# Routed experts on one core: the search for the k-th score, the first row lists and the row gathers, in another order

## What is computed

```python
h = _layernorm(x) * (1 + ca) + sa
x = x + ga * causal_mean(h)              # softmax over an all-zero causal mask
h = _layernorm(x) * (1 + cb) + sb        # the token rows, here called h2
x = x + gb * ffn(h)
# ffn: 8 experts, width 128 -> 512 -> 128, gelu
scores = softmax(xf @ gate_weight.T).T                       # 8 x 4096
vals, idx = top_k(scores.reshape(-1), 2 * S)                 # the 8192 best pairs
gate = zeros(8, S).at[idx // S, idx % S].add(vals)
out = einsum('es,esd->sd', gate, y) + shared                 # y: each expert's output
```

## Time and profile before

| | us |
|---|---|
| median of 3 runs (404.95 to 410.02) | 405.38 |
| the profiled execution | 403.75 |
| its span in the profile | 402.0 |
| busy: PE / DVE / ACT / POOL | 297.1 / 168.1 / 138.1 / 209.7 |
| POOL, scatters L779 (72) | 113.5 |
| POOL, gathers L766 (72) | 69.9 |

### The profile page before, as it was taken

One profiled execution on the slowest core, in us unless ns is written; L12 is line 12 of the kernel. 1 busy time (PEld: TensorE's weight loads), 2 busy tenths in 40 slices (PEclk: granted clock), 3 DMA queues, 4 the chain that ended last, 5 costly groups with the idle time before them and its releaser, 6 DMA issues.

```text
span 402.0 us, 4835 instructions
## 1 busy us (share of the span) xinstructions
PE 297.1 (74%) x1158; PEld 162.7 (40%) x1158; DVE 168.1 (42%) x774; ACT 138.1 (34%) x228; POOL 209.7 (52%) x216
## 2 busy tenths in 40 slices
PE   1647667799999699998776977679786897669500
PEld 1536657653334344544332543335343344234200
DVE  2777748247775860244344213442144323211200
ACT  2135546743334235433233333233232333233200
POOL 2333443100000065037878788787888788786662
PEclk9998665569999999999899889898899989898955
DMA  8907200230000095044455554555445555342331
GB/s 231 294 2 201 62 27 30 68 48 0 27 28 27 26 277 147 28 127 87 76 118 126 105 102 82 115 126 106 100 82 119 125 103 104 74 73 27 30 34 13
DMA packets 49886, 35.96 MB, mean 89 GB/s; under 512 B 7816, under 2 KB 44479, under 8 KB 49855
## 3 DMA queue, kind: packets, MB, share of 16 engines
q0 software_dynamic: 13824, 14.46, 21.1%
q1 hardware_dynamic: 35792, 20.73, 18.5%
q10 hardware_dynamic: 238, 0.42, 0.4%
HBM read 23.65 MB, written 11.94 MB: 89 GB/s over the span
## 4 chain that ended last, share of the span: by engine, by line
POOL 34%; PE 23%; issue 17%; DMA 11%; DVE 11%; ACT 1%; SPq 1%; POOLq 0%; DVEq 0%; ACTq 0%
POOL out_dram L779 23%; POOL R L766 9%; PE Y L916 8%; DMA out_dram<-YO,IDXB 8%; PE U L892 7%; DVE R L434 2%; DMA XW<-in_L_attn_x_dram 2%; DVE ST L400 2%; PE U L898 2%; PE R1b L810 1%; DVE R L442 1%; DVE R L448 1%; PE R L810 1%; PE LG L855 1%; PE LG L922 1%
## 5 line engine op out<-in xcount | busy, mean ns | idle before, releaser
L779 POOL DMA_INDIRECT out_dram<-YO,IDXB x72 | 113.5, 1576 | 31.0 <-issue 20.7
L766 POOL DMA_INDIRECT R<-rows_scratch,IDXB x72 | 69.9, 971 | 105.5 <-DVE IDXB L655 68.9
L335 ACT ACTIVATE HF<-U,CB 128x512 f32<-128x512 f32 x72 | 49.5, 687 | 100.3 <-PE U L898 100.3
L916 PE MATMUL Y<-HF,XW 128*128 128x512 f32 x144 | 83.1, 664 | 0.0
L898 PE MATMUL U<-XT,XW 128*128 128x512 f32 x144 | 78.9, 631 | 0.7 <-issue 0.7
L689 DVE SCALAR_TENSOR_TENSOR YO<-R1b,GT,R 128x128 f32<-128x128 f32 x72 | 20.3, 344 | 122.4 <-PE R1b L810 122.4
L810 PE MATMUL R<-CST,R 128*128 128x128 f32 x104 | 21.5, 343 | 40.6 <-DMA R<-rows_scratch,IDXB 39.9
L898 PEld LDWEIGHTS U<-XT,XW 128*128 128x128 f32 x144 | 29.7, 208 | 39.6 <-issue 39.6
L810 PEld LDWEIGHTS R<-CST,R 128*128 128x128 f32 x104 | 15.0, 173 | 54.7 <-DMA R<-rows_scratch,IDXB 51.5
L892 PE MATMUL U<-H2F,WS 128*128 128x512 f32 x64 | 36.7, 663 | 0.0
L335 ACT ACTIVATE HF<-U,COL 128x512 f32<-128x512 f32 x32 | 22.0, 687 | 42.5 <-PE U L892 42.2
(11 more groups left out here) (136 smaller groups left out, 357.6 us busy)
## 6 DMA issues: line engine op xcount, KB each, us to landing
XW<-in_L_ffn_W_dram SPq DMA_DIRECT2D x36, 256.0 KB, 3.1
XW<-in_L_attn_x_dram SPq DMA_DIRECT2D x8, 256.0 KB, 7.1
rows_scratch<-GBC SPq DMA_DIRECT2D x2, 1024.0 KB, 7.3
rows_scratch<-HT SPq DMA_DIRECT2D x8, 256.0 KB, 2.4
out_dram<-SHO SPq DMA_DIRECT2D x8, 256.0 KB, 2.3
R<-rows_scratch,IDXB POOLq DMA_INDIRECT x72, 2.8
out_dram<-YO,IDXB POOLq DMA_INDIRECT x72, 3.3
INV<-in_inv_dram SPq DMA_DIRECT2D x4, 256.0 KB, 6.4
```

The source lines that it names most:

```text
L335: eng.activation(HF[:, g % RING, :], UB[g % 2][:, :], ACT.Gelu_apprx_tanh, bias=bias).then_inc(M["a_gelu"], 1)
L766: eng.indirect_dma_start(XG[:, v % XR, s, :], None, rows_dram, bass.IndirectOffsetOnAxis(ap=IDXB[:, v, s:s + 1], axis=0)).then_inc(M[f"ld_ ...
L779: eng.indirect_dma_start(out, bass.IndirectOffsetOnAxis(ap=IDXB[:, v, s:s + 1], axis=0), YO[:, v % 2, s, :], None, compute_op=ALU.add).the ...
L916: eng.matmul(bank[:, :], down_weights(g), HF[:, g % RING, :], start=c == 0, stop=c == NC - 1).then_inc(M["pe_dn"], 1)
```

## The change

1. **POOL's order in the block loop**: `rstd(0, j+3)` stands where `rstd(0, j+2)` stood, so the statistics of a block's first norm are finished one round earlier.
2. **End of the block loop**: block 7 is turned first in round 7; `turn_h2` and `rows_out` of blocks 5, 6, 7 move into the search (steps 3, 5, 7); block 7's second norm goes from ACT to DVE (`norm2_last`) and its transposes to bank R2; the softmaxes cover blocks 0 to 4 and 5 to 7, in halves, and both exponentials stand together.
3. **Search** begins a half-step earlier (BIT0 = 2), `close` of the shared blocks moves to steps 21 to 35 (behind the first lists), with TMP of 5 places instead of 2.
4. **Ties** go by half-steps right behind the last bit; a prefix tile CX with a leading zero column takes the place of two subtractions; a difference is taken by PE (NEGI) instead of DVE; the count column is the 129th column of DQ.
5. **Lists**: unit 0 in two halves, units 1 to 8 four half-steps apart, then v+8 during unit v.
6. **Gathers**: XR = 10; 36 of them (nine units) before the first scatter, then two after each scatter of units 0 to 9, four after units 10 to 13.
7. **In a unit**, `yt` and `xt` stand together at the third step; `ye` and `copy_x` as well. Expert weights load at steps 20, 23, 26, 29.

```diff
@@ constants @@
-XR = 5
+XR = 10
+AHEAD = 9
-BIT0 = 3
+BIT0 = 2
-TIE0 = max(BIT_AT) // 2 + 1
+H0 = max(BIT_AT) + 1
+K_MASK, K_TIE, K_CUM, K_DQ, K_IDX = 0, 1, 2, 5, 6
+MASK_AT = {K_IDX - 2 + 4 * v: v for v in range(1, AHEAD)}
+LOAD_AT = {(H0 + K_IDX) // 2 + 1 + 3 * i: i for i in range(WR)}
+CLOSE_AT = {21: 0, 23: 1, 25: 2, 27: 3, 29: 4, 31: 5, 33: 6, 35: 7}
+ROWS_AT = {3: NB - 3, 5: NB - 2, 7: NB - 1}
+def gathered(v):
+    return min(max(NT * AHEAD + PER_GAP * (v + 1), NT * (v + 5)), NT * NU)
@@ scalar, block loop @@
-            for j in range(NB + 2):
+            for j in range(NB):
...
+            norm2(NB - 2)
+            affine2(NB - 2)
+            affine2(NB - 1)
+            expo(0)
             expo(1)
@@ vector @@
+            softmax(0, 0)
             stats2(NB - 1)
...
-            softmax(0)
-            softmax(1)
+            norm2_last()
+            softmax(0, 1)
+            softmax(1, 0)
+            softmax(1, 1)
@@ vector, ties @@
-                    eng.tensor_tensor(RK, CUMX, bank[:, 256:512], ALU.subtract).then_inc(M["v_tie"], 1)
+                    eng.tensor_tensor(RK, CX[:, 0:256], bank[:, 0:256], ALU.add).then_inc(M["v_tie"], 1)
...
-                    eng.tensor_tensor(CUMX[:, 1:256], EQ[:, 1:256], EQ[:, 0:255], ALU.subtract).then_inc(M["v_dq"], 1)
@@ vector, unit loop @@
-                        if v + 3 < NU:
-                            idx_mask(v + 3)
+                        if v >= 1 and v + AHEAD - 1 < NU:
+                            idx_mask(v + AHEAD - 1)
@@ gpsimd @@
-            for j in range(1, NB + 1):
-                rstd(1, j - 1)
-                if j + 2 < NB:
-                    rstd(0, j + 2)
+            for j in range(NB + 1):
+                if j:
+                    rstd(1, j - 1)
+                if j + 3 < NB:
+                    rstd(0, j + 3)
...
+            for q in range(gathered(-1)):
+                gather(q // NT, q % NT)
+            eng.wait_ge(M["v_used"], 1)
+            used = eng.value_load(USED[0:1, 0:1], min_val=UMIN, max_val=NU)
+            for v in range(NU):
+                scatter(v)
+                for q in range(gathered(v - 1), gathered(v)):
+                    gather(q // NT, q % NT)
@@ tensor, unit loop @@
+                    if c == 2:
+                        if 0 <= v - 1 < NU:
+                            yt(v - 1)
+                        if v + 1 < NU:
+                            xt(v + 1)
```

More of the change, by code:

```diff
@@ L142, in adaln_moe @@
         SCT = sb("SCT", [P, NB * NT * E])
-        TK = sb("TK", [P, 5, NB * NT * E])
-        SEL, GT, EQ, CUMX, RK = (TK[:, i, :] for i in range(5))
+        TK = sb("TK", [P, 5 * 256 + 2])
+        SEL, GT, RK = (TK[:, i * 256:(i + 1) * 256] for i in range(3))
+        EQ0, EQ = TK[:, 768:1024], TK[:, 769:1025]
+        CX = TK[:, 1025:1282]
+        NEGI = sb("NEGI", [P, P])
         CNT = sb("CNT", [P, 2], F16)
@@ L233, in sync @@
             for s in range(NSTEP):
-                g = on_step(s - LAG - 2)
-                if g is not None and g < GS0 and g % NC == NC - 1:
-                    b = g // NC
+                if s in CLOSE_AT:
+                    b = CLOSE_AT[s]
                     eng.wait_ge(M["v_out"], b + 1)
@@ L422, in norm1, with norm2_last @@
                 m.then_inc(M["v_xn"], 1)
+            def norm2_last():
+                b = NB - 1
+                eng.wait_ge(M["g_rs2"], NB)
+                eng.wait_ge(M["v_ag2"], NB)
+                eng.wait_ge(M["pe_t4"], NB - 2)
+                for t in range(NT):
+                    m = eng.tensor_scalar(XN2[:, b % 2, t, :], X2[:, b, t * P:(t + 1) * P], MV[:, 1, b, t, 0:1],
+                                          RS[:, 1, b, 0, t:t + 1], ALU.subtract, ALU.mult)
+                m.then_inc(M["v_xn2"], 1)
             def prefix(b):
@@ L476, in softmax @@
                 mx, sm, rc = (RED[:, i, t0:t1] for i in range(3))
[L477 to L481, removed]
+                if half == 0:
+                    eng.wait_ge(M["pe_lg"], NB if part else PART0)
+                    k = step("v_tk", eng.tensor_reduce(mx, logits, AX_X, ALU.max))
+                    eng.wait_ge(M["v_tk"], k)
+                    eng.tensor_tensor(ex, logits, mx.unsqueeze(2).to_broadcast([P, n, E]),
+                                      ALU.subtract).then_inc(M["v_sub"], 1)
+                    return
                 eng.wait_ge(M["a_exp"], part + 1)
@@ L691, in yo, with half_step @@
                     m.then_inc(M["v_yo"], 1)
+            def half_step(h):
+                if h in BIT_AT:
+                    bit(BIT_AT[h])
+                elif h >= H0:
+                    ties(h - H0)
             eng.wait_ge(M["v_sc"], 2)
@@ L695, in vector @@
             for s in range(NSTEP):
-                if 2 * s in BIT_AT:
-                    bit(BIT_AT[2 * s])
-                g = on_step(s - LAG - 2)
-                if g is not None and g < GS0 and g % NC == NC - 1:
-                    close(g // NC)
-                if 0 <= s - TIE0 <= XT_STEP:
-                    ties(s - TIE0)
-                if 2 * s + 1 in BIT_AT:
-                    bit(BIT_AT[2 * s + 1])
-                if s == TIE0 + XT_STEP:
+                half_step(2 * s)
+                if s in CLOSE_AT:
+                    close(CLOSE_AT[s])
+                half_step(2 * s + 1)
+                if s == UNIT1 - 1:
                     eng.wait_ge(M["v_used"], 1)
@@ L866, in tensor @@
             turn_x(0)
-            for j in range(NB + 2):
+            for j in range(NB):
                 if j + 1 < NB:
                     turn_x(j + 1)
+                if j == NB - 1:
+                    turn_x2(j)
                 if j == 2:
@@ L1002, in tensor @@
                     down(g)
-                g = on_step(s - LAG - 2)
-                if g is not None and g < GS0 and g % NC == NC - 1:
-                    close(g // NC)
-                if 0 <= s - TIE0 <= XT_STEP:
-                    ties(s - TIE0)
-                if 2 * s + 1 in BIT_AT:
-                    bit(BIT_AT[2 * s + 1])
-                if s == TIE0 + XT_STEP:
+                if s in CLOSE_AT:
+                    close(CLOSE_AT[s])
+                half_step(2 * s + 1)
+                if s in ROWS_AT:
+                    turn_h2(ROWS_AT[s])
+                if s == UNIT1 - 1:
                     eng.wait_ge(M["v_used"], 1)
```

325 lines of the change are left out of this document (170 added, 155 removed).

## The result

| | us |
|---|---|
| changed kernel, median of 4 runs (376.61 to 378.19) | 377.19 |
| kernel before, median of 4 runs (404.52 to 410.02) | 405.16 |
| ratio | 0.930, 95% interval 0.923 to 0.937 |
| predicted (range) | 359.0 (348 to 370) |

What follows compares the result with a forecast made beforehand. POOL's queue bounds the kernel: its start and the work left at the first scatter decide. 70.0+34.1+11.0+45.7=160.8, then +101.0+50.6+28.7+14.7=355.8 us of span, hence 359 us, range 348 to 370.

Steps and rivals of the forecast that it cites:

- Block loop: Start of kernel: all five DVE waits for POOL go, last prefix scan at 51.6 us, first bit at 70.0, gain 17.6.
- search: From first to last bit: three closes leave it, so it takes 34.1 us instead of 36.2, last bit at 104.1.
- ties: Ties and first list, after the last bit: 11.0 us instead of 18.0, first gather at 115.1 us.
- PE at half level did not bind the block loop: Rival: PE, or DVE through it, keeps the block loop from shortening; first bit 81.0, time 370 us; chance 0.09.
- the thirty-six gathers: POOL before the first scatter: 36 x 1.27 = 45.7 us, lists every 4.4 us, first scatter at 160.8 us.
- an idle of POOL before the first scatter of under 2 us: Sign asked for in POOL's timeline: first scatter near 161 us, with under 2 us of idle before it.
- The pitches: Unit stage on POOL: ten gaps of 10.1 us, four of 12.64, three of 9.55, together 101.0 + 50.6 + 28.7.
- PE never sets the pitch: Rival: PE sets the pitch of the first ten gaps, 11.0 us a unit, time 368 us; chance 0.13.
- the slower one: Rival: PE stays at half clock through the unit stage, 18.8 us a unit, 495 us; chance 0.02.
- No mask held a gather: Rival: DVE's masks hold gathers in the first nine units, costing 5.5 us, time 364.5 us; chance 0.03.
- the lock rule: Skill's rule for gathers beside DVE masks: shared port lock delays GpSimd's DMA, about 3100 ns for a 620 ns transfer.
- The tail: From the last unit's first scatter to the span's end: 14.7 us, taken from the trace before.

Runs made afterwards that it cites:

- the third group: Runs on the second group's chip, including the changed kernel unaltered: 363.5 us, 0.9005 of the kernel before, without a late counter update.
- sixteen_first: Changed kernel with 16 gathers before the first scatter and four behind each, instead of 36 first: 386.9 us.
- twelve_first: Changed kernel with 12 gathers before the first scatter and four behind each, instead of 36 first: 400.5 us, and 405.5 us when repeated.
- before_again: The kernel before, unaltered, run again for its trace beside the altered kernels: 403.8 us in the fourth group of runs.

## Why the prediction was right and wrong

**Block loop, search, ties: right.** First bit 67.4 to 67.7 and, with the best clock, 66.8 in the changed kernel's traces, at the lower bound of 67.6 and below it (70.0 predicted); PE at half level did not bind the block loop, and that rival falls. The search took 34.2 to 36.0 (34.1): with a clock of 0.79 and 0.86 from 63 to 75 us it was 34.2, with 0.57 it was 36.0, as before. First bit and search together miss by 0.4 with 0.57. The ties and the first list took 11.4 (11.0).

**The step that failed: the thirty-six gathers ("They take 36 x 1.27 = 45.7 us, to 160.8", with a list every 4.4 us).** In the timed runs POOL stood still 11.2 us for lists and 5.7 for unit 0. But the sum itself was right when nothing is held: in the traces without holds the lists come 4.4 us apart to the tenth (118.3, 122.7, 127.1, 131.5, 135.9, 140.3), the stream takes 45.4 us and the first scatter comes at 159.2 to 161.0. There the kernel takes 361.4 to 364.4, inside the range. What the step took for granted is that an increment arrives when the operation ends. With holds those of PE arrive up to 5.9 us late by the modelled ends (the 7 us in the expectations is how long ACT stood idle, 6.76). DVE's additions wait for PE's transposes, PE's list products for DVE's masks behind those additions, and ACT's gelus for PE's products, so PE, DVE and ACT stop together; POOL then runs dry or ends its stream, twelve times in the three traces with holds, and each time a burst of increments begins 1.2 to 1.9 us after its last gather; a few come in singly inside the stream, such as those of 127.95 and 130.75. That the end of the stream lets them in is inferred from this order in time. Fewer instructions get done, and many increments have no record: from 120 to 132 us the trace with holds has 31 instructions that end with an increment and 12 of these increments as updates; the one without has 53 and 52. Two of the signs that the prediction asked for failed here: "36 in a row with 0.30 between them", and an idle of POOL before the first scatter of under 2 us, which was 5.66. That the time without holds lies in the range does not make up for this: the forecast had no term, no rival and no chance for such a state.

What the holds are is not shown. Not the amount of traffic, nor the stores or loads (each was there without holds), nor the chip. That increments are missing from the record in the same stretches makes the recording itself a suspect: the Trainium skill (NOTIFIC — the notification-queue block, "Overflow: three behaviours, one of which stalls the engine") describes a path for trace records that drops records when its ring is full in one mode, and stalls the engine that makes them in another; the modes are alternatives. The trace agrees only in part. Records do go missing where time is held. But from 180 to 212 us of the same trace, among the units, 29 of 103 increments are missing too (none of 110 in the trace without holds), and there the pitches are 10.1 and nothing is late: what loses records does not by itself hold time. All timed runs here are profiled, so it can't be told whether the held time exists without the profiler. Nor was the kernel before traced in a group with holds.

**The pitches: right, with two terms too small.** Without holds the ten gaps take 263.63 - 159.96 = 103.7 (101.0): seven are 10.12 to 10.23, but the first, the second and the tenth take 10.84, 10.49 and 11.23, since there the landing of the scatter before is later than two gathers cover (1.01 and 1.42 of wait). The four long ones take 50.6 (50.6), the last three 29.7 (28.7) for the same reason. PE never sets the pitch, so that rival falls, and PE at half clock through the units, the slower one, as well: its clock is 1.00 from 113 to 260 us, and 0.84 from 260 to 340 us, where PE has time to spare. No mask held a gather: in the trace of the third group the 14 gathers that overlap with a mask take 973 ns on average and the other 58 974, against 971 before; so the trace still doesn't bear out the lock rule.

**The tail: a term taken from the trace before.** 14.7 was used as it stood; it is 17.0, of which 6.94 against 4.65 is the DRAIN. The change added five counters, and I had looked only at what it added to the queues.

The sum without holds, term by term against the prediction (first scatter, ten gaps, four, three, tail): -0.8 (first scatter) + 2.7 + 0 + 1.0 + 2.3 = 5.2, from 355.8 to the 360.9 of the trace in the third group.

**What the parts bring.** The kernel before, too, has 16 gathers ahead of its first scatter (12 and 4 in its order above). So `sixteen_first` is the change without the 20 further gathers; `twelve_first`, which its expectation calls "the gathers of the kernel before", has a unit less of lead than that kernel. With 16 the time is 386.9 against 403.3: the first scatter comes 20 us earlier (160.70, and 180.98 in `before_again`), the pitch is the same, and the tail is longer. The 20 further gathers bring 23 us more, 1.2 each, nearly their own length of 1.27. With only 12, the earlier start brings nothing (400.5 against 404.1, 405.5 against 403.8), because PE's waits for its rows give it all back. Whether the kernel before with 12 would lose as much was not run.

## What to carry to other kernels

Work moved ahead of a queue's first due item is worth its full length on that queue, but only with a lead that its consumers can live with; check the lead first. Before an experiment's gain is believed, run the unchanged kernel in the same group: here a single run showed 13 us that belonged to the moment. And a kernel's fixed end is not fixed: landing counters of POOL's queue have a price there, and one counter can serve several buffers if each new round waits for the one before.

## What the runs showed of the hardware that I had not expected

Increments of PE can arrive up to 5.9 us after the modelled end of the product, in bursts, while gathers follow each other: in two of six groups of runs (the timed one among them), and not in a later group on one of the same chips. No increment of DVE or ACT stands late in the three traces with holds. SP lost time there without waiting for a counter (3.45 us for what takes 1.15). POOL's last DRAIN takes 4.65 us in the kernel before and 2.69, 4.98 and 6.94 with two, five and ten landing counters for the gathers. The Trainium skill (VectorE: DVE Perf Modes, "The DRAIN you can't avoid") gives some 12 ns, constant, for such a DRAIN at the ends of a program on all five engines; those of SP, ACT, DVE and PE take 3 to 17 ns here, POOL's takes microseconds, and the measurement decides.
